# Routing stage of a Mamba, attention and mixture-of-experts block: inverse softmax sums spread by repeated DMA loads instead of by TensorE

## The chip, the cores and the metric

The kernel runs on one core of a Trainium2 chip. The metric is the time of one execution on the device in microseconds (us); lower is better. The time before is the median of three runs, 3432.8 us (3429.8 to 3436.05).

The core's engines are TensorE (PE in the profile, its weight loads PEld), VectorE (DVE), ScalarE (ACT), GpSimd (POOL) and SyncE (SP). SP's queue issues nearly all DMA transfers here; GpSimd's queue issues the indirect ones.

## The reference, cut to what matters

The input `x` is 2 batches of 2048 tokens of 256 channels. It is normalised, and goes through a Mamba block and through a transformer layer with a top-1 mixture of 8 experts; both results are added to `x`. The changed part lies in the transformer layer, between attention and the experts:

```python
attn = jax.nn.softmax(scores, axis=-1)
o = jnp.einsum('bhqk,bhkd->bhqd', attn, v)          # 16 heads of 16 channels
o = o.transpose(0, 2, 1, 3).reshape(b, s, h)
x = x + (o @ wo + bo)
hn2 = _layernorm(x, ln2_g, ln2_b).reshape(-1, h)
logits = hn2 @ gate_w + gate_b
idx = jnp.argmax(logits, axis=-1)                    # one expert for each token
...
moe = y[idx, jnp.arange(hn2.shape[0])]
return x + moe.reshape(b, s, h)
```

## The kernel before

Five stages follow each other, each closed by a barrier of all engines: projection of q, k and v; Mamba; attention; routing (`phase_route`, the changed function); experts.

**What attention leaves.** It works on items, one for each batch, group of 4 heads and block of 512 tokens: 2 x 4 x 4 = 32. For each item it writes a 128x512 block to `oraw_d` in DRAM: for each of the 4 heads 16 rows of unnormalised output and, in the seventeenth row, the softmax sums. Its end also loads the sums of the first 28 items (`SUMS_KEPT`), inverts them and stores them to `rs_d`, 4 rows of 512 for each item. The last 4 items (`LATE`) are left to the routing stage.

**Routing** handles 8 chunks of 512 tokens (`NCH`); `c` is the chunk. The channels are on the partitions (`OT[c]`, 128 partitions, 2 halves `k`, 512 tokens).

- SP, `load_o(c)` (L1398 to L1404): four DMAs of 128 KB, one for each half `k` and each group `g`, each from 4 heads x 16 rows x 512 to 64 partitions x 512. They signal `o_in[c % RING]`, `RING` being 4.
- SP, `load_inverses` (L1406 to L1410): one 32 KB DMA for each batch and group puts the stored inverses into `INV`, 16 partitions (one for each head). The four inverses of the late items are loaded as sums (`SS`), inverted by VectorE (L1626) and copied into `INV` by four small DMAs (L1424).
- TensorE, `spread(c)` (L1480 to L1489): two fp32 products of the selection matrix `SEL` (made by GpSimd, 1 where the channel belongs to the head) with `INV[:, c, :]` repeat each head's inverses over its 16 channels, in the PSUM tile `pS`. Each fp32 product shows as two matmul records.
- VectorE, `scale(c)` (L1574 to L1577): `OT[c] = pS * OT[c]`.
- TensorE, `project(c)` (L1491 to L1499): `OT[c]` times `WO` into `pA`.
- VectorE, `stats(c)` (L1579 to L1589): `pA` plus `XN[c]`, then mean and variance; `normalise(c)` gives `HN`.
- GpSimd, `base(c)` (L1461 to L1463): `XB[c] += XN[c]`, a 128x1024 tensor_tensor in SBUF.
- TensorE `turn` and `gate`, VectorE `choose` (L1601 to L1614): logits, largest logit, one-hot choice of expert. TensorE `count` and VectorE `place` (L1616 to L1622): the slot of each token in its expert's list.
- GpSimd, `scatter(c)` (L1465 to L1470): four indirect DMAs, each of which writes 128 token numbers of 4 bytes to computed slots of `ids_d`.
- SP stores `HN` to `hn_d` and `XB[c]` to `base_d`, 512 KB each in rows of 1 KB.

**Order.** Each engine's order is written out by hand. VectorE: scale(0), inversion of the late sums, then for each c: stats(c), place(c-2), scale(c+1), normalise(c), choose(c-1). TensorE: for each c: project(c+1), spread(c+2), turn(c), count(c-1), gate(c). GpSimd: base(c), scatter(c-1). SP: loads of chunks 0 to 2 (`AHEAD` is 3) with the inverses between them, a wait for the inverted late sums, then for each c: load_o(c+3), a wait for `hn_done` (c), store of `HN`, a wait for `base_done` (c), store of `XB`. The stage ends when all stores and scatters have landed.

Of the kernel before, what the change touches and what calls it, by code (L numbers as in the profile page):

```python
# [33 lines left out]
GH = 4  # L34
# [1286 lines left out]
def phase_route(nc, kept, oraw_d, rs_d, ids_d, hn_d, base_d, TE, TR, batches):  # L1321
# [11 lines left out]
    LATE = ITEMS - SUMS_KEPT  # L1333
    O_IN = 16 * 4
    AHEAD = 3
    with ExitStack() as ctx:
# [5 lines left out]
        OT = [m.sb(f"ot{c}", [P, KC, BANK]) for c in range(NCH)]  # L1342
        SEL = m.sb("sel", [HEADS, KC, P])
        INV = m.sb("inv", [HEADS, NCH, BANK])
        HN = [m.sb(f"hn{n}", [P, TG, C]) for n in range(2)]
# [15 lines left out]
        CMP = m.sb("cmp", [P, NTL, NE])  # L1361
        pA = m.ps("pA", [P, TG, C])
        pS = m.ps("pS", [P, KC, BANK])
        pT = [m.ps(f"pT{n}", [P, 2, KC, P]) for n in range(2)]
# [5 lines left out]
        inverted = m.sem("inverted")  # L1370
        inv_in = m.sem("inv_in")
        late_in = m.sem("late_in")
        s_ps = m.sem("s_ps")
        o_in = [m.sem(f"o_in{n}") for n in range(RING)]
# [19 lines left out]
        with nc.Block() as block:  # L1394

            @block.sync
            def _(sp):
                def load_o(c):  # L1398
                    b, cb = divmod(c, NB)
                    for k in range(KC):  # L1400
                        for g in range(2):
                            raw = oraw_d[b * GB * NB + (2 * k + g) * NB + cb].rearrange("(h r) q -> h r q", r=P // GH)
                            half = slice(g * GH * HD, (g + 1) * GH * HD)
                            sp.dma_start(OT[c][half, k, :], raw[:, 0:HD, :]).then_inc(o_in[c % RING], 16)  # L1404

                def load_inverses(b, g):  # L1406
                    first = (b * GB + g) * NB
                    sp.dma_start(INV[g * GH:(g + 1) * GH, b * NB:(b + 1) * NB, :],
                                 rs_d[first * GH:(first + NB) * GH, :].rearrange("(c h) q -> h c q", h=GH)
                                 ).then_inc(inv_in, 16)  # L1410

                sp.dma_start(SS[:, :], oraw_d[SUMS_KEPT:ITEMS].rearrange("i (h r) q -> (i h) r q", r=P // GH)[:, HD, :]
                             ).then_inc(sums_in, 16)
                for g in range(GB):
                    load_inverses(0, g)
                load_o(0)
                for b in range(1, batches):
                    for g in range(GB - (b == batches - 1)):
                        load_inverses(b, g)
                load_o(1)  # L1420
                load_o(2)
                sp.wait_ge(inverted, 1)
                for i in range(LATE):
                    sp.dma_start(INV[HEADS - GH:HEADS, NCH - LATE + i, :], SS[i * GH:(i + 1) * GH, :]  # L1424
                                 ).then_inc(late_in, 16)
                for c in range(NCH):
                    if c + AHEAD < NCH:
                        if c + AHEAD >= RING:
                            sp.wait_ge(scaled, c + AHEAD - RING + 1)
                        load_o(c + AHEAD)  # L1430
                    rows = slice(c * BANK, (c + 1) * BANK)
                    sp.wait_ge(hn_done, c + 1)
                    sp.dma_start(hn_d[rows, :].rearrange("(t p) c -> p t c", p=P), HN[c % 2][:, :, :]
                                 ).then_inc(hn_out[c % 2], 16)
                    sp.wait_ge(base_done, c + 1)
                    sp.dma_start(base_d[rows, :].rearrange("(t p) c -> p t c", p=P), XB[c][:, :, :]).then_inc(base_out, 16)
                for n in range(2):
                    sp.wait_ge(hn_out[n], 16 * (NCH // 2))
                sp.wait_ge(base_out, 16 * NCH)

            @block.gpsimd
            def _(pool):
                make_identity(pool, ident, id_ready)
                pool.memset(SEL[:, :, :], 1.0).then_inc(id_ready, 1)
                pool.wait_ge(id_ready, 3)
                pool.affine_select(out=SEL[:, :, :], in_=SEL[:, :, :], compare_op=ALU.is_gt, fill=0.0, base=1,
                                   pattern=[[P, KC], [1, P]], channel_multiplier=-HD).then_inc(id_ready, 1)
                pool.wait_ge(id_ready, 4)
                pool.affine_select(out=SEL[:, :, :], in_=SEL[:, :, :], compare_op=ALU.is_gt, fill=0.0, base=HD,
                                   pattern=[[-P, KC], [-1, P]], channel_multiplier=HD).then_inc(id_ready, 1)  # L1450
                pool.iota(IDT[:, :], pattern=[[P, NCH * TG]], base=0, channel_multiplier=1).then_inc(consts, 1)
# [27 lines left out]
            def _(pe):  # L1479
                def spread(c):  # L1480
                    if c >= 1:
                        pe.wait_ge(scaled, c)
                    if c == 0:
                        pe.wait_ge(inv_in, 16 * (GB * batches - 1))
                    if c == NCH - LATE:
                        pe.wait_ge(late_in, 16 * LATE)
                    for k in range(KC):
                        mm = pe.matmul(pS[:, k, :], SEL[:, k, :], INV[:, c, :], start=True, stop=True)
                    mm.then_inc(s_ps, 1)  # L1489

                def project(c):  # L1491
                    pe.wait_ge(scaled, c + 1)
                    if c >= 1:
                        pe.wait_ge(x1_done, c)
                    for t in range(TG):
                        for k in range(KC):
                            mm = pe.matmul(pA[:, t, :], OT[c][:, k, t * P:(t + 1) * P], WO[:, k, :],
                                           start=(k == 0), stop=(k == KC - 1))
# [30 lines left out]

                pe.wait_ge(id_ready, 5)  # L1530
                spread(0)
                project(0)
                spread(1)
                pe.wait_ge(consts, 8)
                for c in range(NCH):
                    if c + 1 < NCH:
                        project(c + 1)
                    if c + 2 < NCH:
                        spread(c + 2)
                    turn(c)  # L1540
# [20 lines left out]
            def _(dve):  # L1561
# [12 lines left out]
                def scale(c):  # L1574
                    dve.wait_ge(o_in[c % RING], O_IN * (c // RING + 1))
                    dve.wait_ge(s_ps, c + 1)
                    dve.tensor_tensor(OT[c][:, :, :], pS[:, :, :], OT[c][:, :, :], ALU.mult).then_inc(scaled, 1)  # L1577

                def stats(c):  # L1579
                    dve.wait_ge(a_ps, c + 1)  # L1580
                    dve.tensor_tensor(XN[c][:, :, :], pA[:, :, :], XN[c][:, :, :], ALU.add).then_inc(x1_done, 1)
                    dve.wait_ge(x1_done, c + 1)
# [383 lines left out]
```

## Time and profile before

| | |
|---|---|
| median of 3 runs | 3432.8 us (3429.8 to 3436.05) |
| the profiled execution | 3432.8 us |
| its span | 3431.2 us |
| TensorE busy | 2923.5 us, 85% |
| VectorE busy | 2602.2 us, 76% |
| ScalarE busy | 1711.8 us, 50% |
| GpSimd busy | 929.5 us, 27% |
| routing stage | 2939.1 to 3078.7 us |

The profile is one execution. Times within it are us from the start of its span. A row of the timeline gives start, duration, engine, line of the kernel, what is written and read, shape and count; what stands in brackets behind it is how long the engine was idle before it, and what ended that. The clock given with a window is the one granted to TensorE, as a share of full speed. The DMA share is the mean busy share of the core's 16 DMA engines; GB/s is what they moved together. A DMA's landing is the time from its issue to its last signal.

### The profile page before, as it was taken

The page shows a single profiled execution, that of the slowest core. Times are in us where ns is not written, and L with a number is a line of the kernel's source. Part 1 is how long each engine was busy: PE and PEld are TensorE (multiplying, and loading weights), DVE is VectorE, ACT ScalarE, POOL GpSimd, SP SyncE. Part 2 cuts the span into 40 slices and gives each one's busy share as a digit, 9 for nine tenths or more (in the row PEclk, how much of TensorE's full clock was granted, in tenths as well). Part 3 has the DMA queues.
Part 4 walks back from the last instruction along what each step waited for, and adds up shares of the span by engine and source line. Part 5 has one row for each costly group of instructions (what it writes and reads, how often), then busy time and mean ns, then how long its engine had stood idle before and what let it go on. Part 6 is the DMA issues. An engine that isn't in the chain of part 4 may idle for free. (4 is left out here: it accounts for less than half of the span.)

```text
span 3431.2 us, 42905 instructions
## 1 busy us (share of the span) xinstructions
PE 2923.5 (85%) x12700; PEld 1390.8 (41%) x12700; DVE 2602.2 (76%) x3764; ACT 1711.8 (50%) x2099; POOL 929.5 (27%) x530
## 2 busy tenths in 40 slices
PE   5768697897977877699899999999999999759998
PEld 3433243343433423333333333333333333448887
DVE  5426898998988999588898988889888996462222
ACT  2325545545546454056676766667666777211110
POOL 2203554555545556300000000000000000143443
PEclk9879899998999988689999999999999999769999
DMA  4542111212111111755445555435554430355663
GB/s 148 171 136 81 62 74 56 81 68 74 68 68 68 68 50 55 94 66 79 70 63 82 66 85 78 63 63 74 78 85 64 63 46 7 81 100 196 201 206 122
DMA packets 215985, 296.83 MB, mean 87 GB/s; under 512 B 117806, under 2 KB 162376, under 8 KB 201310
## 3 DMA queue, kind: packets, MB, share of 16 engines
q1 hardware_dynamic: 203262, 264.30, 35.8%
q0 software_dynamic: 12512, 29.82, 3.0%
q8 instruction: 120, 1.97, 0.3%
q14 instruction: 91, 0.75, 0.1%
HBM read 241.40 MB, written 57.56 MB: 87 GB/s over the span
## 5 line engine op out<-in xcount | busy, mean ns | idle before, releaser
L736 DVE TENSOR_REDUCE attn_mx<-attn_pX 128x1 f32<-128x512 f32 x2048 | 1271.8, 683 | 183.4 <-PE attn_pX L642 181.6
L714 ACT ACTIVATE attn_pr<-attn_pS 128x1024 f32<-128x1024 f32 x1024 | 992.6, 1022 | 524.1 <-PE attn_pS L655 523.4
L642 PE MATMUL attn_pX<-attn_ks,attn_qs 48*128 48x512 f32 x2048 | 754.1, 494 | 76.5 <-DMA attn_vs<-v_d 25.4
L1186 PE MATMUL mamba_pY<-mamba_g,mamba_ident 128*128 128x512 f32 x1024 | 530.5, 667 | 203.8 <-DVE mamba_g L1312 203.2
L1299 DVE TENSOR_TENSOR_SCAN mamba_h<-mamba_pA,mamba_hs,mamba_db 128x512 f32<-128x512 f32 x512 | 617.7, 1264 | 66.4 <-ACT mamba_pA L1045 65.7
L642 PEld LDWEIGHTS attn_pX<-attn_ks,attn_qs 48*128 48x128 f32 x2048 | 306.9, 192 | 780.0 <-DVE attn_mx L736 714.9
L1045 ACT ACTIVATE mamba_pA<-mamba_dt,mamba_an 128x512 f32<-128x512 f32 x512 | 351.7, 691 | 497.8 <-DVE mamba_h L1299 497.6
L982 POOL TENSOR_TENSOR mamba_db<-mamba_bq,mamba_u 128x2048 f32<-128x2048 f32 x128 | 579.3, 4526 | 71.3 <-DVE mamba_u L1259 71.0
L665 PE MATMUL attn_pO<-attn_pr,attn_vs 128*17 128x512 f32 x4096 | 556.6, 616 | 0.4 <-ACT attn_pr L714 0.4
L655 PE MATMUL attn_pS<-attn_qs,attn_ks 50*128 50x512 f32 x2048 | 471.4, 416 | 52.3 <-DMA attn_qs<-attn_mt 33.5
L1186 PEld LDWEIGHTS mamba_pY<-mamba_g,mamba_ident 128*128 128x128 f32 x1024 | 213.2, 214 | 504.5 <-DVE mamba_g L1312 260.0
L1312 DVE TENSOR_TENSOR mamba_g<-mamba_h,mamba_bq 128x2048 f32<-128x2048 f32 x128 | 294.0, 2297 | 7.8
L655 PEld LDWEIGHTS attn_pS<-attn_qs,attn_ks 50*128 50x128 f32 x2048 | 255.6, 192 | 90.9 <-issue 54.2
L623 POOL DMA_DIRECT2D rows_xn<-xn_d x8 | 6.1, 767 | 1018.1 <-PE attn_pO L665 1018.1
L1115 PE MATMUL mamba_pP<-mamba_xt,mamba_wc 128*128 128x512 f32 x512 | 227.0, 597 | 22.9 <-DVE mamba_an L1284 22.9
L1864 DVE TENSOR_SCALAR exp_hm<-exp_pH,exp_b 128x256 f32<-128x256 f32 x46 | 22.3, 484 | 234.6 <-PE exp_pH L1802 234.6
L1828 ACT ACTIVATE exp_hm<-exp_pH,exp_b 128x256 f32<-128x256 f32 x46 | 21.8, 475 | 320.7 <-PE exp_pH L1802 320.7
L1802 PE MATMUL exp_pH<-exp_xt,exp_w 128*128 128x256 f32 x736 | 165.0, 383 | 1.1 <-DVE exp_xt L1843 1.1
L1815 PE MATMUL exp_pY<-exp_w,exp_hm 128*128 128x256 f32 x736 | 162.7, 379 | 0.0
L1115 PEld LDWEIGHTS mamba_pP<-mamba_xt,mamba_wc 128*128 128x128 f32 x512 | 97.7, 191 | 147.9 <-issue 147.9
L966 POOL TENSOR_TENSOR mamba_hs<-mamba_h,mamba_mk 128x4 f32<-128x4 f32 x126 | 25.2, 200 | 483.8 <-DVE mamba_g L1312 483.8
L1802 PEld LDWEIGHTS exp_pH<-exp_xt,exp_w 128*128 128x128 f32 x736 | 141.4, 192 | 21.1 <-DVE exp_xt L1843 1.5
(190 smaller groups left out, 2076.2 us busy)
## 6 DMA issues: line engine op xcount, KB each, us to landing
mamba_bq<-bc_d SPq DMA_DIRECT2D x64, 1024.0 KB, 4.7
attn_ks<-parts_d SPq DMA_DIRECT2D x192, 256.0 KB, 8.7
exp_w<-in_w SPq DMA_DIRECT2D x46, 1024.0 KB, 5.5
attn_vs<-v_d SPq DMA_DIRECT2D x32, 544.0 KB, 15.6
parts_d<-proj_qp SPq DMA_DIRECT2D x32, 512.0 KB, 3.0
attn_qs<-parts_d SPq DMA_DIRECT2D x192, 64.0 KB, 8.3
attn_qs<-attn_mt SPq DMA_DIRECT2D x512, 1.0 KB
oraw_d<-attn_oe SPq DMA_DIRECT2D x32, 256.0 KB, 2.1
```

Source lines behind the costliest of these rows:

```text
L642: pe.matmul(pX[bank(s, n)][:, :], QS[slot][rows, pair, qt * P:(qt + 1) * P], KS[slot][rows, pair, part * BANK:(part + 1) * BANK], start=Tr ...
L655: mm = pe.matmul(pS[pair][:, h, :], KS[slot][rows, pair, kt * P:(kt + 1) * P], QS[slot][rows, pair, :], start=True, stop=True)
L665: mm = pe.matmul(pO[32 * h:32 * h + VW, :], VS[s][:, kt, h, :], PR[2 * (kt % 2) + h // 2][:, h % 2, :], start=(kt == 0), stop=(kt == KT - 1))
L714: act.activation(PR[2 * (kt % 2) + pair][:, :, :], pS[pair][:, :, :], ACT.Exp, scale=HD ** -0.5).then_inc(p_sb, 1)
L736: dve.tensor_reduce(MX[:, col:col + 1], pX[bank(s, n)][:, :], AX.X, ALU.max).then_inc(x_max, 1)
L982: pool.tensor_tensor(DB[k % 2][:, :, :], BQ[q % 2][:, 0, :, :], U[s][:, j, :].unsqueeze(1).to_broadcast([P, QN, BANK]), ALU.mult).then_inc ...
L1045: act.activation(pA[n % 2][:, :], DT[s][:, j, :], ACT.Exp, scale=AN[:, j, q * QN + n:q * QN + n + 1]).then_inc(da_done, 1)
L1115: mm = pe.matmul(bank(s, place)[0:rows, :], w, x, start=(i == 0), stop=(i == len(pairs) - 1))
L1186: mm = pe.matmul(pY[j][:, :], ident[:, :], G[k % 2][:, n, :], start=False, stop=(q == NQ - 1 and n == QN - 1))
L1299: dve.tensor_tensor_scan(H[k % 2][:, n, :], pA[n % 2][:, :], DB[k % 2][:, n, :], HS[:, j, q * QN + n:q * QN + n + 1], ALU.mult, ALU.add).t ...
L1312: dve.tensor_tensor(G[k % 2][:, :, :], H[k % 2][:, :, :], BQ[q % 2][:, 1, :, :], ALU.mult).then_inc(hc_done, 1)
L1802: mm = pe.matmul(pH[n][:, f % 2, :], W1[s][:, k, f * P:(f + 1) * P], XT[s][:, k, :], start=(k == 0), stop=(k == KC - 1))
```

## The change

- `load_inverses`, `INV`, `SEL`, the PSUM tile `pS`, `spread` and the four small copies of late inverses are gone.
- A new `load_r(c)` on SP's queue: four DMAs for each chunk, one for each half `k` and group `g`. Each reads the 4 rows of inverses of one item from `rs_d`, repeats each 16 times (a stride of zero in the second dimension) and writes 64 partitions x 512, 128 KB, into a new SBUF tile `SM[c]`. They signal the same semaphore as `load_o(c)`, so scale waits for eight DMAs (`O_IN = 16 * 8`).
- The late sums are inverted in `SS` as before, and then stored to `rs_d` by one 32 KB DMA. SP waits for it before `load_r(4)`, the first chunk of batch 1.
- `scale(c)` is `OT[c] = OT[c] * SM[c]`, both operands in SBUF.
- SP loads 2 chunks ahead instead of 3. The load of the late sums comes after the eight DMAs of chunk 0 instead of first.
- `pA` has two buffers, and `project(c)` waits for the sum of chunk c-2 instead of c-1.

```diff
@@ phase_route, constants and tiles
     LATE = ITEMS - SUMS_KEPT
-    O_IN = 16 * 4
-    AHEAD = 3
+    O_IN = 16 * 8
...
-        SEL = m.sb("sel", [HEADS, KC, P])
-        INV = m.sb("inv", [HEADS, NCH, BANK])
+        SM = [m.sb(f"sm{c}", [P, KC, BANK]) for c in range(NCH)]
...
-        pA = m.ps("pA", [P, TG, C])
-        pS = m.ps("pS", [P, KC, BANK])
+        pA = [m.ps(f"pA{n}", [P, TG, C]) for n in range(2)]
@@ SP
-                def load_inverses(b, g):
-                    first = (b * GB + g) * NB
-                    sp.dma_start(INV[g * GH:(g + 1) * GH, b * NB:(b + 1) * NB, :],
-                                 rs_d[first * GH:(first + NB) * GH, :].rearrange("(c h) q -> h c q", h=GH)
-                                 ).then_inc(inv_in, 16)
-
+                def load_r(c):
+                    b, cb = divmod(c, NB)
+                    for k in range(KC):
+                        for g in range(2):
+                            i = b * GB * NB + (2 * k + g) * NB + cb
+                            half = slice(g * GH * HD, (g + 1) * GH * HD)
+                            sp.dma_start(SM[c][half, k, :], rs_d[i * GH:(i + 1) * GH, :].unsqueeze(1)
+                                         .to_broadcast([GH, HD, BANK])).then_inc(o_in[c % RING], 16)
+
+                load_o(0)
+                load_r(0)
                 sp.dma_start(SS[:, :], oraw_d[SUMS_KEPT:ITEMS].rearrange("i (h r) q -> (i h) r q", r=P // GH)[:, HD, :]
                              ).then_inc(sums_in, 16)
-                for g in range(GB):
-                    load_inverses(0, g)
-                load_o(0)
-                for b in range(1, batches):
-                    for g in range(GB - (b == batches - 1)):
-                        load_inverses(b, g)
                 load_o(1)
-                load_o(2)
+                load_r(1)
                 sp.wait_ge(inverted, 1)
-                for i in range(LATE):
-                    sp.dma_start(INV[HEADS - GH:HEADS, NCH - LATE + i, :], SS[i * GH:(i + 1) * GH, :]
-                                 ).then_inc(late_in, 16)
+                sp.dma_start(rs_d[SUMS_KEPT * GH:ITEMS * GH, :], SS[:, :]).then_inc(inv_out, 16)
                 for c in range(NCH):
-                    if c + AHEAD < NCH:
-                        if c + AHEAD >= RING:
-                            sp.wait_ge(scaled, c + AHEAD - RING + 1)
-                        load_o(c + AHEAD)
+                    if c + 2 < NCH:
+                        if c + 2 >= RING:
+                            sp.wait_ge(scaled, c + 3 - RING)
+                        load_o(c + 2)
+                        if c + 2 == NB * (batches - 1):
+                            sp.wait_ge(inv_out, 16)
+                        load_r(c + 2)
@@ GpSimd
-                pool.memset(SEL[:, :, :], 1.0).then_inc(id_ready, 1)
...
@@ TensorE
-                def spread(c):
...
-                    for k in range(KC):
-                        mm = pe.matmul(pS[:, k, :], SEL[:, k, :], INV[:, c, :], start=True, stop=True)
-                    mm.then_inc(s_ps, 1)
-
                 def project(c):
                     pe.wait_ge(scaled, c + 1)
-                    if c >= 1:
-                        pe.wait_ge(x1_done, c)
+                    if c >= 2:
+                        pe.wait_ge(x1_done, c - 1)
@@ VectorE
                 def scale(c):
                     dve.wait_ge(o_in[c % RING], O_IN * (c // RING + 1))
-                    dve.wait_ge(s_ps, c + 1)
-                    dve.tensor_tensor(OT[c][:, :, :], pS[:, :, :], OT[c][:, :, :], ALU.mult).then_inc(scaled, 1)
+                    dve.tensor_tensor(OT[c][:, :, :], OT[c][:, :, :], SM[c][:, :, :], ALU.mult).then_inc(scaled, 1)
```

## Rows read from the trace of the kernel before

**Rows 1.** The page: busy time, a load of the mamba stage

```profile
PE 2923.5 (85%) x12700; PEld 1390.8 (41%) x12700; DVE 2602.2 (76%) x3764; ACT 1711.8 (50%) x2099; POOL 929.5 (27%) x530
...
mamba_bq<-bc_d SPq DMA_DIRECT2D x64, 1024.0 KB, 4.7
```

**Rows 2.** Windows inside the routing stage: start:end, length, busy us (instructions), clock, DMA, GB/s

```profile
core 0: us, PE busy (x) PEld busy (x) DVE busy (x) ACT busy (x) POOL busy (x), PEclk, DMA share, GB/s
2936.00:2955.00 19.00, 3.75 (x4) 1.16 (x4) 0.54 (x4) 1.28 (x1) 2.27 (x10) 0.60 0.28 95
3000.00:3045.00 45.00, 41.50 (x178) 31.80 (x177) 42.41 (x123) 7.13 (x18) 24.93 (x20) 0.77 0.70 113
2970.00:2973.00 3.00, 3.00 (x11) 1.97 (x10) 0.80 (x1) 0.00 (x0) 0.00 (x0) 0.92 1.02 335
```

**Rows 3.** Waits in the routing stage: line, what it waited for, us, times, longest

```profile
PE route_pS L1488 <- DMA route_inv<-rs_d: 15.7, 1, 15.7
DVE route_ot L1577 <- PE route_pS L1488: 15.2, 1, 15.2
```

**Rows 4.** Timeline of the routing stage: start us, us, engine, line, work [idle before]

```profile
2950.81 3.75 PE L1488 MATMUL route_pS<-route_inv,route_sel 16*128 16x512 f32 x4 [15.73 <-DMA route_inv<-rs_d]
...
2954.66 1.23 DVE L1577 TENSOR_TENSOR route_ot<-route_pS,route_ot 128x1024 f32<-128x1024 f32 x1 [15.24 <-PE route_pS L1488]
...
2987.06 1.23 DVE L1577 TENSOR_TENSOR route_ot<-route_pS,route_ot 128x1024 f32<-128x1024 f32 x1
...
3036.96 1.22 DVE L1577 TENSOR_TENSOR route_ot<-route_pS,route_ot 128x1024 f32<-128x1024 f32 x1
...
3038.24 5.41 PE L1497 MATMUL route_pA<-rows_wo,route_ot 128*128 128x256 f32 x16
...
3041.68 2.92 DVE L1610 TENSOR_TENSOR route_oh<-route_wtt,route_mw 128x32 f32<-128x32 f32 x1
3042.17 2.36 POOL L1463 TENSOR_TENSOR rows_xb<-rows_xb,rows_xn 128x1024 f32<-128x1024 f32 x1
```

**Rows 5.** Timeline of the end of the routing stage

```profile
3045.51 1.22 DVE L1581 TENSOR_TENSOR rows_xn<-route_pA,rows_xn 128x1024 f32<-128x1024 f32 x1
...
3062.79 0.17 DVE L1622 CAST route_slot<-route_slf 128x4 int32<-128x4 f32 x1
...
3078.70 0.21 POOL L92 MEMSET exp_ident<- 128x128 f32 x1 [10.68 <-POOLq L1394]
```

**Rows 6.** DMA of 2944 to 2959 us: busy tenths in slices, total, issues

```profile
DMA  2232222222222222222222222222222222222222
...
DMA packets 760, 1.45 MB, mean 97 GB/s; under 512 B 54, under 2 KB 54, under 8 KB 759
...
route_ot<-oraw_d SPq DMA_DIRECT2D x8, 128.0 KB
```

**Rows 7.** Timeline of SP's DMA issues in the routing stage

```profile
2939.14 0.34 SPq L1412 DMA_DIRECT2D route_ss<-oraw_d  x1
...
2990.67 0.36 SPq L1433 DMA_DIRECT2D hn_d<-route_hn  x1
...
3007.53 10.73 SPq L1404 DMA_DIRECT2D route_ot<-oraw_d  x4
...
3032.07 0.36 SPq L1436 DMA_DIRECT2D base_d<-rows_xb  x1
```

**Rows 8.** DMA issues near 2969, 2990 and 3032 us: count, KB, us to landing

```profile
hn_d<-route_hn SPq DMA_DIRECT2D x1, 512.0 KB, 3.0
base_d<-rows_xb SPq DMA_DIRECT2D x1, 512.0 KB, 4.4
...
hn_d<-route_hn SPq DMA_DIRECT2D x1, 512.0 KB, 17.1
...
base_d<-rows_xb SPq DMA_DIRECT2D x1, 512.0 KB, 8.0
```

**Rows 9.** Groups of instructions, page part 5: busy us, mean ns, idle before

```profile
L1312 DVE TENSOR_TENSOR mamba_g<-mamba_h,mamba_bq 128x2048 f32<-128x2048 f32 x128 | 294.0, 2297 | 7.8
```

More of the change, by code:

```diff
@@ L1370, in phase_route @@
         inverted = m.sem("inverted")
-        inv_in = m.sem("inv_in")
-        late_in = m.sem("late_in")
-        s_ps = m.sem("s_ps")
+        inv_out = m.sem("inv_out")
         o_in = [m.sem(f"o_in{n}") for n in range(RING)]
@@ L1443, in _ @@
                 make_identity(pool, ident, id_ready)
-                pool.memset(SEL[:, :, :], 1.0).then_inc(id_ready, 1)
[L1445 to L1450, printed above, removed]
                 pool.iota(IDT[:, :], pattern=[[P, NCH * TG]], base=0, channel_multiplier=1).then_inc(consts, 1)
@@ L1479, in _ @@
             def _(pe):
-                def spread(c):
-                    if c >= 1:
[L1482 to L1486, printed above, removed]
-                    for k in range(KC):
-                        mm = pe.matmul(pS[:, k, :], SEL[:, k, :], INV[:, c, :], start=True, stop=True)
-                    mm.then_inc(s_ps, 1)
                 def project(c):
                     pe.wait_ge(scaled, c + 1)
-                    if c >= 1:
-                        pe.wait_ge(x1_done, c)
+                    if c >= 2:
+                        pe.wait_ge(x1_done, c - 1)
                     for t in range(TG):
                         for k in range(KC):
-                            mm = pe.matmul(pA[:, t, :], OT[c][:, k, t * P:(t + 1) * P], WO[:, k, :],
+                            mm = pe.matmul(pA[c % 2][:, t, :], OT[c][:, k, t * P:(t + 1) * P], WO[:, k, :],
                                            start=(k == 0), stop=(k == KC - 1))
@@ L1528, in count @@
                     pe.matmul(pN[:, c % 2, 0:TG, :], LOWER[:, :], OH[:, :, :], start=False, stop=True).then_inc(n_ps, 1)
-                pe.wait_ge(id_ready, 5)
-                spread(0)
                 project(0)
-                spread(1)
+                pe.wait_ge(id_ready, 2)
                 pe.wait_ge(consts, 8)
@@ L1537, in _ @@
                         project(c + 1)
-                    if c + 2 < NCH:
-                        spread(c + 2)
                     turn(c)
@@ L1575, in scale @@
                     dve.wait_ge(o_in[c % RING], O_IN * (c // RING + 1))
-                    dve.wait_ge(s_ps, c + 1)
-                    dve.tensor_tensor(OT[c][:, :, :], pS[:, :, :], OT[c][:, :, :], ALU.mult).then_inc(scaled, 1)
+                    dve.tensor_tensor(OT[c][:, :, :], OT[c][:, :, :], SM[c][:, :, :], ALU.mult).then_inc(scaled, 1)
                 def stats(c):
                     dve.wait_ge(a_ps, c + 1)
-                    dve.tensor_tensor(XN[c][:, :, :], pA[:, :, :], XN[c][:, :, :], ALU.add).then_inc(x1_done, 1)
+                    dve.tensor_tensor(XN[c][:, :, :], pA[c % 2][:, :, :], XN[c][:, :, :], ALU.add).then_inc(x1_done, 1)
                     dve.wait_ge(x1_done, c + 1)
```

## The prediction

> **What bounds the kernel now.** I read the page first, for the shares of the engines and to find the stage [rows 1]. The changed function is the routing stage, from 2939.1 us, where SP issues its first load [rows 7], to 3078.7 us, where the expert stage begins [rows 5]: 140 us of 3431. Everything behind it starts when it ends, so a shift of its end moves the end of the kernel one for one, if the stages on either side keep their length; they are not touched.
>
> Second, the list of waits. Multiplying the raw attention output by the inverse sums (scale, L1577) waits once, 15.2 us, and TensorE's spreading of the inverses (L1488) waits once, 15.7 us, for the loads of the inverses [rows 3]. After the first chunk scale is never late for data.
>
> Third, the timeline. scale starts at 2954.66, the fourth at 2987.06 and the eighth at 3036.96 [rows 4]: 49.9 us for four chunks, 12.5 us each. In that stretch VectorE is busy 42.4 of 45 us and the DMA engines 70% [rows 2], so VectorE sets the pace, with DMA close behind. Part of its busy time is a stall: a 128x32 operation at L1610 shows 2.92 us while GpSimd runs a 2.36 us tensor_tensor beside it [rows 4]. From the last scale to the last slot (L1622) it is 25.8 us, and from there to the next stage 15.9 us [rows 4, 5]: scatter, its landing, the barrier.
>
> Fourth, the DMA view, which decides this case. From 2944 to 2959 us, loads of raw output are queued back to back, and yet the sixteen engines are busy only two to three tenths and carry 97 GB/s [rows 6]. When the stores of a chunk flow, from 2970 to 2973 us, all engines are busy and carry 335 GB/s [rows 2]. With twelve loads queued the share does not rise, so these loads share the same quarter of the engines, four of them, and go one behind another. A 128 KB load costs 131 KB / 97 GB/s = 1.35 us, a chunk of four 5.4 us. The Trainium skill (DMA: Bandwidth & Descriptors, on why a DMA increments its semaphore by 16) says the number of engines is the largest up to 16 that divides the outermost sizes of both sides, and that they are the lowest-numbered; here the source's outermost size is 4 heads. The trace's quarter share agrees.
>
> **The change, part by part.**
>
> Removed on TensorE: 32 spreading matmuls and their selection matrix. TensorE is not what VectorE waits for after the first chunk [rows 3], so its gain is nothing, hidden under VectorE. Removed from DMA: seven 32 KB loads of inverses and four of 8 KB; at 97 GB/s the seven are 7 x 0.34 = 2.4 us.
>
> Moved on VectorE: scale takes both operands from SBUF. L1312, two SBUF operands of 2048 elements, takes 2.30 us [rows 9]; half the elements are near the 1.22 us that scale takes now [rows 4]. I take no difference; the bounds are 0 and +1.1 us per chunk, of which only the last chunk's counts if DMA sets the pace. Such a scale may meet GpSimd's 2.36 us operation, but L1610 pays for that today, and one operation pays for it either way. A second accumulator in PSUM frees project from the sum before it; no wait on that is among those that matter, so nothing.
>
> Added on DMA: for each chunk, four more loads of 128 KB, each four rows of inverses repeated sixteen times, 32 in all. Their source has the same outermost 4 and their target the same 64 partitions as the loads of raw output. I price them alike, 1.35 us on the same four engines. The nearest row the other way is the broadcast load of the mamba stage, 1 MB in 4.7 us [rows 1], which uses all engines, but its outermost size is the 128 partitions; it shows that repeated reads of a row are not slow or especially cheap. The rule of the Trainium skill cited above would put the new loads on four engines too; by it the sum is the one below, and by the mamba row it would be that of the second rival.
>
> Sum on the four engines, in the order of SP's queue. First, the latency that isn't transfer: the wait for inverses ends at 2950.81 [rows 4], 11.7 us after the first issue at 2939.14 [rows 7]; in between lie four loads of output (5.4) and seven of inverses (2.4), so 3.9 us are start and completion. In the changed kernel the eight loads of chunk 0 land at 2939.1 + 3.9 + 8 x 1.35 = 2953.8, 0.9 us ahead of today's first scale. The loads of chunk 7 stand behind 56 others and behind the stores of chunks 0 to 4, because SP's program issues chunk c+2's loads before chunk c's stores. The stores of a chunk are 2 x 524 KB / 335 GB/s = 3.1 us on every engine [rows 2]; undisturbed they land in 3.0 and 4.4 us [rows 8]. So chunk 7 lands at 2939.1 + 3.9 + 64 x 1.35 (86.4) + 5 x 3.1 (15.5) + 0.3 for the two 32 KB transfers of sums = 3045.2, against 3036.96: +8.2 us. The pace, 10.8 + 3.1 = 13.9 us, is now DMA's, not VectorE's 12.5. A prefetch of two chunks instead of three costs nothing more, since the queue of the four engines is never empty.
>
> The tail: VectorE no longer lags behind. Today the eighth x + projection (L1581) starts 8.55 us after its scale, 2.7 of it the stall at L1610. With 1.3 us for scale and 5.4 for the projection [rows 4] it could start after 6.9 us: -1.6 us, bounds -1.7 and 0. Undisturbed sum: +6.6 us.
>
> Disturbed: the stores slow down once the indirect scatter (L1468) is under way. Chunk 2's store, issued at 2990.67, takes 17.1 us, and chunk 5's, issued at 3032.07, lands 8.0 us later, at 3040.1 [rows 7, 8]. In these 49.4 us the four engines carry four pairs of stores (12.5) and two chunks' loads (10.8), 23.3 us of work: 26 us too much, up to 6.5 per pair. SP too is held: four issues last 10.7 us from 3007.53 [rows 7]. In the changed kernel the pairs of chunks 1 to 4 reach the four engines just when the loads of a chunk have landed, about 14 us after the previous ones; the slots of an earlier chunk are ready some 12 us after its landing, so scatter and stores meet four times. Bounds 0 and 4 x 6.5 = 26 us. I take about half, 3.4 us each, +13.6, because twelve of sixteen engines will have done their stores earlier and a scatter comes once in 17 us instead of 12.5. Total +20 us.
>
> Queued behind SP's longer issue are the stores; normalise waits for a store two chunks back, which lies ahead of the loads that normalise's predecessor already waited for, so no new wait. The new wait of SP for the stored late inverses comes before chunk 4, some 30 us after that store; free.
>
> The profiled execution is 3432.8 us, 1.6 above its span and equal to the median of the runs. **Forecast 3453 us**, own range 3443 to 3466 (+10 to +33).
>
> **The rivals.** Bound for all: 0.2%, 6.9 us, is about what a measurement of this kernel tells from no change.
> A. Stores and scatter don't add: only the undisturbed sum, +5 to +9, 3440 us. For it: twelve engines write earlier than today. Against: chunk 2's 17.1 us [rows 8].
> B. Faster: the repeated rows go over all sixteen engines, as the mamba broadcast does. A chunk's loads are then 5.4 + 1.35 = 6.8 us, chunk 0 lands at 2949.8, 4.9 us earlier than today's first scale, and VectorE's 12.5 us pace again decides, as long as loads, stores and disturbance stay under it: chunk 7 lands at 2939.1 + 3.9 + 54.4 + 15.8 + at most 26 = 3039 at the latest, 3026 at half. -5 to -6 us with the tail, 3427 us. Against: the outermost size.
> C. No change: the sixteen reads of one row cost under 0.98 us per load, so a chunk is 5.4 + 3.9 + 3.1 < 12.5 us and VectorE keeps the pace; start and pace as today, 3433 us. Against: 1 MB in 4.7 us gives no rate above the usual one.
> D. The disturbance grows with the traffic, reads included: above +33, 3470 us.
>
> **Numbers.** Forecast 0.62, A 0.12, B 0.08, C 0.08, D 0.10. A straddles the bound, 0.07 slower and 0.05 same. Slower 0.79, same 0.13, faster 0.08. The range 3436 to 3468 leaves out B, C and part of D.
>
> **What would show it.** In the changed profile: scale waits for a DMA at nearly every chunk; DMA from 2941 to about 2965 us stays at a quarter share and 97 GB/s; scale starts at 2954, then every 14 us and more after the fourth; VectorE's busy share in the stage falls; TensorE has no L1488 work. Wrong would be: a share well above a quarter in the first 20 us (B), scale intervals of 12.5 us (B or C), or of 13.9 us throughout (A).

## The result, and the profile after

The changed kernel takes 3466.8 us (median of 4 runs, 3464.8 to 3471.9), the kernel before, run beside it, 3434.4 us (3429.8 to 3438.9). The ratio is 1.0097, 95% interval 1.0079 to 1.0115: slower by 32.4 us. The profiled execution of after took 3471.8 us (span 3470.2), 39.0 us more than that of before. Of this, 4.0 us lie ahead of the changed stage, in code that is the same: its first load is issued at 2943.14 us instead of 2939.14. The stage itself is 174.9 us long instead of 139.6: +35.3 us. From here on a start is told after the stage's first issue ("rel."), so that the 4.0 us do not get in the way.

Rows of the timeline of after that answer to [rows 4, 5] (start, us, engine, line, work, idle before and releaser):

```profile
2956.90 1.23 DVE L1549 TENSOR_TENSOR route_ot<-route_ot,route_sm 128x1024 f32<-128x1024 f32 x1 [13.47 <-DMA route_sm<-rs_d]
...
2967.69 1.23 DVE L1549 TENSOR_TENSOR route_ot<-route_ot,route_sm 128x1024 f32<-128x1024 f32 x1 [0.56 <-DMA route_sm<-rs_d]
...
2990.26 1.07 POOL L1456 DMA_INDIRECT ids_d<-route_idt,route_slot  x1 [10.98 <-DVE route_slot L1594]
...
2991.75 1.23 DVE L1549 TENSOR_TENSOR route_ot<-route_ot,route_sm 128x1024 f32<-128x1024 f32 x1 [1.79 <-DMA route_sm<-rs_d]
...
3023.76 1.23 DVE L1549 TENSOR_TENSOR route_ot<-route_ot,route_sm 128x1024 f32<-128x1024 f32 x1 [19.23 <-DMA route_sm<-rs_d]
...
3074.35 3.75 DVE L1549 TENSOR_TENSOR route_ot<-route_ot,route_sm 128x1024 f32<-128x1024 f32 x1 [4.79 <-DMA route_sm<-rs_d]
3074.67 2.35 POOL L1451 TENSOR_TENSOR rows_xb<-rows_xb,rows_xn 128x1024 f32<-128x1024 f32 x1
...
3084.80 1.22 DVE L1553 TENSOR_TENSOR rows_xn<-route_pA,rows_xn 128x1024 f32<-128x1024 f32 x1 [2.17 <-PE route_pA L1474]
...
3102.09 0.17 DVE L1594 CAST route_slot<-route_slf 128x4 int32<-128x4 f32 x1
...
3117.99 0.21 POOL L92 MEMSET exp_ident<- 128x128 f32 x1 [10.67 <-POOLq L1389]
```

The first four scales come 10.8, 11.5 and 12.5 us apart (rel. 13.8, 24.6, 36.1, 48.6; before 15.5, 26.3, 36.7, 47.9 by the same reading). Then there are 32.0 us to the fifth, and VectorE idles 19.23 us of it for a load. The first scatter of slots, at 2990.26, stands just ahead of this gap. The last row of scale is three times as long as the others, beside GpSimd's operation of 2.35 us.

The waits of the stage, against [rows 3]:

```profile
PE route_pA L1474 <- DVE route_ot L1549: 76.8, 8, 21.9
...
DVE route_ot L1549 <- DMA route_sm<-rs_d: 51.2, 7, 19.2
```

Seven of eight scales wait for the repeated loads, 51.2 us in all, where before one waited, for TensorE. Windows of the stage, against [rows 2] (the last one has the limits of the window shown there):

```profile
core 0: us, PE busy (x) PEld busy (x) DVE busy (x) ACT busy (x) POOL busy (x), PEclk, DMA share, GB/s
2943.00:2962.00 19.00, 3.82 (x11) 3.18 (x12) 4.71 (x6) 1.28 (x1) 1.21 (x7) 0.52 0.25 87
2962.00:2992.00 30.00, 19.33 (x91) 16.02 (x89) 19.71 (x66) 4.48 (x11) 6.13 (x4) 0.83 0.42 152
2992.00:3023.00 31.00, 9.82 (x44) 8.21 (x44) 11.81 (x35) 2.14 (x5) 11.18 (x9) 0.61 0.34 70
...
3000.00:3045.00 45.00, 17.59 (x87) 15.03 (x86) 20.00 (x66) 4.28 (x10) 12.52 (x10) 0.66 0.35 98
```

From 3000 to 3045 VectorE was busy 42.4 us before and is 20.0 us now; the DMA engines' share fell too, from 0.70 to 0.35. In the gap (2992 to 3023) loads are queued all the time, and only 70 GB/s move, less than half of the stretch ahead of it. So the stage waits for DMA while DMA moves little and is not out of work. The DMA view of 2944 to 2962 us (against [rows 6]) and of 2992 to 3004 us:

```profile
DMA  0301222222244222222222222222222222222222
...
DMA packets 872, 1.66 MB, mean 92 GB/s; under 512 B 64, under 2 KB 64, under 8 KB 871
```

```profile
DMA  3222591129800000101911900500000001080004
GB/s 96 96 96 102 94 61 48 61 77 41 14 0 1 0 0 0 24 24 34 55 48 41 14 7 27 20 0 0 0 0 14 21 27 34 27 27 27 20 27 14
DMA packets 380, 0.40 MB, mean 33 GB/s; under 512 B 109, under 2 KB 266, under 8 KB 380
...
hn_d<-route_hn SPq DMA_DIRECT2D x1, 512.0 KB, 26.4
```

The first is the quarter share of four engines with repeated loads among the others. The second is what adding up bandwidths does not show: a third of that rate, with slices near nothing, and a store that lands after 26.4 us. SP is held as well (timeline of SP around that stretch, against [rows 7]):

```profile
2985.47 5.76 SPq L1399 DMA_DIRECT2D route_ot<-oraw_d  x4
2991.28 7.32 SPq L1407 DMA_DIRECT2D route_sm<-rs_d  x4
2998.64 7.11 SPq L1428 DMA_DIRECT2D hn_d<-route_hn  x1
3005.80 9.85 SPq L1431 DMA_DIRECT2D base_d<-rows_xb  x1
3015.69 7.39 SPq L1399 DMA_DIRECT2D route_ot<-oraw_d  x4
```

The first two rows are the eight loads of the fifth chunk (chunk 4). SP has issued the last of them by 2998.60, and the fifth scale starts at 3023.76, 25 us later. So this gap does not come from a late issue, though the scatters stand ahead of `base` in GpSimd's order, and SP waits for `base`.

### The profile page after: what moved, and what is told of

Read it like the earlier page. It is cut to its first block and busy times, and to the rows that moved or that the text cites. A ratio compares the mean times of both kernels' runs of the same rounds, so it can differ in the third digit from the quotient of the medians.

```text
span 3470.2 us, 42850 instructions
## 1 busy us (share of the span) xinstructions
PE 2911.1 (84%) x12668; PEld 1388.7 (40%) x12668; DVE 2599.9 (75%) x3764; ACT 1710.9 (49%) x2099; POOL 927.4 (27%) x527
## 5 line engine op out<-in xcount | busy, mean ns | idle before, releaser
L982 POOL TENSOR_TENSOR mamba_db<-mamba_bq,mamba_u 128x2048 f32<-128x2048 f32 x128 | 579.3, 4526 | 73.1 <-DVE mamba_u L1259 72.8
L1115 PEld LDWEIGHTS mamba_pP<-mamba_xt,mamba_wc 128*128 128x128 f32 x512 | 97.9, 191 | 147.2 <-issue 147.2
## 6 DMA issues: line engine op xcount, KB each, us to landing
attn_vs<-v_d SPq DMA_DIRECT2D x32, 544.0 KB, 15.5
```

The costliest lines, as they stand in the source:

```text
L982: pool.tensor_tensor(DB[k % 2][:, :, :], BQ[q % 2][:, 0, :, :], U[s][:, j, :].unsqueeze(1).to_broadcast([P, QN, BANK]), ALU.mult).then_inc ...
L1115: mm = pe.matmul(bank(s, place)[0:rows, :], w, x, start=(i == 0), stop=(i == len(pairs) - 1))
```

## The experiments

All starts are in us after the stage's first issue; "tail" is from the eighth scale to the first instruction of the next stage. Each median stands against runs of the kernel before on the same chip: 3434.4 us for after, 3438.7 for r16 to late_after, 3439.0 for b_ahead1 to r16_ahead3, 3441.9 for shift to distinct. The ratio is an estimate of its own and not quite the quotient of the two medians (or16: 1.0131 against 1.0145). The times within the stage are from one profiled execution of each kernel.

| kernel | median us | ratio to before (95%) | first scatter | longest gap between scales | eighth scale | tail |
|---|---|---|---|---|---|---|
| before | | | 48.3 | 12.5 | 97.8 | 41.7 |
| after | 3466.8 | 1.0097 (1.0079 to 1.0115) | 47.1 | 32.0, 4th to 5th | 131.2 | 43.6 |
| r16 | 3457.3 | 1.0052 (1.0030 to 1.0074) | 44.3 | 34.2, 4th to 5th | 121.7 | 41.9 |
| or16 | 3488.5 | 1.0131 (1.0105 to 1.0157) | 57.9 | 34.8, 3rd to 4th | 152.3 | 40.2 |
| ahead3 | 3467.0 | 1.0079 (1.0058 to 1.0099) | 46.9 | 31.4, 4th to 5th | 131.4 | 41.9 |
| late_after | 3468.1 | 1.0084 (1.0062 to 1.0106) | 112.5 | 13.8 | 102.1 | 68.3 |
| b_ahead1 | 3479.9 | 1.0124 (1.0101 to 1.0146) | 57.3 | 32.9, 4th to 5th | 144.0 | 40.3 |
| late_before | 3464.0 | 1.0064 (1.0048 to 1.0081) | 107.1 | 13.2 | 95.1 | 73.1 |
| no_r | 3442.6 | 1.0010 (0.9998 to 1.0022) | 42.2 | 28.4, 5th to 6th | 106.1 | 41.1 |
| r16_ahead3 | 3455.1 | 1.0046 (1.0030 to 1.0063) | 44.5 | 24.8, 4th to 5th | 119.3 | 42.8 |
| shift | 3476.4 | 1.0107 (1.0085 to 1.0129) | 60.1 | 36.5, 5th to 6th | 134.4 | 43.9 |
| late_store | 3469.1 | 1.0089 (1.0067 to 1.0111) | 46.1 | 30.1, 4th to 5th | 116.6 | 58.8 |
| plain4 | 3507.2 | 1.0191 (1.0173 to 1.0210) | (plain) | 25.8, 4th to 5th | 128.4 | 86.9 |
| distinct | 3488.0 | 1.0137 (1.0113 to 1.0160) | 47.1 | 39.9, 4th to 5th | 150.8 | 43.6 |

**r16 and or16: the loads over all engines.** In r16 a repeated load is cut by head, so that 32 partitions and not 4 rows are its outermost size:

```diff
-   sp.dma_start(SM[c][half, k, :], rs_d[i * GH:(i + 1) * GH, :].unsqueeze(1)
-                .to_broadcast([GH, HD, BANK])).then_inc(o_in[c % RING], 16)
+   for h in range(GH):
+       part = slice((g * GH + h) * HD, (g * GH + h + 1) * HD)
+       sp.dma_start(SM[c][part, k, :], rs_d[i * GH + h:i * GH + h + 1, :]
+                    .to_broadcast([HD, BANK])).then_inc(o_in[c % RING], 16)
```

or16 cuts the loads of the raw output by head too.

> The changed kernel with each repeating load cut into four, one head each (1 row repeated to 16 partitions, outermost size 16); same bytes, same rows, same packets. Theory Q (four engines carry all loads one behind another): these loads spread over all sixteen engines, the four busiest have 5.4 + 1.35 + 3.1 = 9.9 us of work per chunk, VectorE's 12.5 us pace returns; total within -6 to +12 us of before, most of the 32 us gone. Rival R (sixteen reads of the same row are slow in themselves): total stays +20 to +35. Rival S (scale with two SBUF operands, blocked by GpSimd): stays +20 or more.

> As r16, and the loads of raw output cut by head as well: 32 DMAs of 32 KB per chunk, all with outermost size 16. Theory Q: 2.7 us per chunk on every engine, no loads queue up on four; the limit becomes SP's issuing, 32 x 0.33 = 10.6 us per chunk, still under 12.5; total -8 to +8 us of before. Rival R: +20 to +35.

In r16 the first four scales start at 11.6, 22.7, 33.3 and 45.3, 33.7 us for three intervals against 34.8 in the changed kernel, and 2.2 us sooner; then the same gap comes. The total is 18.6 us over before, between the two ranges that were expected. In or16 a chunk has 32 loads, and SP issues one in about 0.46 us: 14.7 us per chunk, and 15.3 is the pace from the first scale on. Cutting finer moved the bound from the four engines to SP. The total, 49.8 us over before, is above both expected ranges: SP's pace had been priced at 10.6 us per chunk, and the gap of 34.8 us behind the first scatter not at all.

**ahead3: three chunks ahead instead of two.** `load_o(2); load_r(2)` are issued ahead of the loop, and the loop loads chunk c+3.

> The changed kernel, loads issued three chunks ahead instead of two. Theory Q: the queue of the four engines is never empty either way, so no difference from the changed kernel: +27 to +38 us. Rival P (the shorter prefetch is what costs): +0 to +12 us.

The eighth scale starts at 131.4 against 131.2, and the total is 28.2 us over before, as the first theory expected. One chunk more of depth is no help here.

**late_after and late_before: the scatters behind everything else.** The same edit on either kernel:

```diff
                 for c in range(NCH):
                     base(c)
-                    if c >= 1:
-                        scatter(c - 1)
-                scatter(NCH - 1)
+                for c in range(NCH):
+                    scatter(c)
```

> The changed kernel, all 32 indirect scatters after the last base instead of one chunk's after each. Theory Q with disturbance by the scatter: eighth scale about 106 us after the first issue of the stage instead of 131, intervals of 13.9 us from the third on; the 41 us of scatters then stand at the end, so the total is about +25 us. If the disturbance comes from the stores alone: eighth scale stays at 125 us or later and the total goes to +45 us.

> The kernel before with all scatters issued after the last base. Theory S: its loads were never in the scatters' way, so the eighth scale moves by less than 2 us from 97.8, the 1 KB store packets of chunks 1 to 7 are quick again (landings of 3 to 5 us instead of 8 to 21), and the scatters that were hidden now stand in the tail: total 10 to 30 us over before (in the change the same move left the total where it was, and 29 us were won ahead of the tail). Rival (the scatters cost the kernel before time in its chunks too): the eighth scale is more than 3 us early.

This pair carries the verdict. Without scatters among its loads the changed kernel has no gap at all: scales at 13.5, 24.4, 35.8, 48.4, 61.7, 75.5, 88.8 and 102.1, the eighth 29.1 us sooner than in after. In the kernel before the same edit wins 2.7 us (97.8 to 95.1), which lies between the under 2 us of the one expectation and the over 3 us of the other. Both totals gain nothing by it, since 32 scatters, one in 1.27 us, now stand behind the last base: the tails grow by 24.7 and 31.4 us. DMA view of late_after from 2990 to 3012 us, about where after had its gap:

```profile
DMA  2224994228982222222222222222599322898222
GB/s 101 101 104 166 395 382 171 101 97 317 384 309 97 97 97 101 97 99 95 93 97 97 99 106 101 101 104 101 209 389 369 121 97 101 313 391 302 97 104 89
DMA packets 2830, 3.73 MB, mean 170 GB/s; under 512 B 115, under 2 KB 1907, under 8 KB 2829
```

Loads at a quarter share and near 97 GB/s, broken by stores at 9 tenths and up to 395 GB/s, and nothing else: this is the undisturbed queue that the prediction added up.

**b_ahead1: the kernel before, one chunk ahead.** `AHEAD = 1`, and the loads of chunks 1 and 2 are no longer issued ahead of the loop. No repeated load is in it.

> The kernel before, but each chunk's rows are asked for one chunk ahead instead of three, so that the loads of chunks 4 to 7 fall behind the first scatter instead of ahead of it. Theory S (what costs the change its time is that its loads run while the scatters of slots write, and the kernel before is spared since its loads are over by then): scales 1 to 4 stay within 2 us of the kernel before (they start 26.3, 36.7, 47.9 and 60.4 us after the first issue), and those after the first scatter come late, the eighth 10 to 30 us later than 97.8; total 3445 to 3470. Theory V (it is the volume: the change moves twice the bytes, and the scatter matters only to a queue that is already full): loads of 5 us per chunk have room for themselves, the eighth scale starts within 5 us of 97.8; total within 0.2% of before.

Its gap of 32.9 us opens at the first scatter and its scale now waits for the load of the raw output (summary of line L1575 of b_ahead1; the kernel before had no such wait [rows 3]):

```profile
L1575 DVE TENSOR_TENSOR route_ot<-route_pS,route_ot x8: 1223/1225/1225, 2957.4 to 3085.8; 128x1024 f32<-128x1024 f32 x8
its engine sat idle before it (us, times) until:
  DMA route_ot<-oraw_d: 45.5, 7
```

So the collision needs no repeated load, and was there to be had in the kernel before. Two parts of the expectation failed. The first four scales did not keep their times: the fourth starts at 59.7 instead of 47.9, so 11.8 of the 46.2 us by which the eighth is late are the shorter prefetch alone, ahead of any scatter. And the total is above its range (3445 to 3470). Nor does this run show what the scatters hit first: between the first one and the fifth scale, 63 of the 1024 store packets of 1 KB take over 1 us (152 of their 228 us), and 11 of the 332 load packets of 2 KB (18 of 52 us). What spared the kernel before is slack: its loads for chunk 6 are issued at 2995.2 us and first used at 3024.5, 29 us later.

**no_r: the changed kernel without its repeated loads.** SM is set to one by VectorE ahead of the first scale, and `load_r` issues nothing, so that the softmax division is left out.

> The changed kernel without its repeated loads: SM is set to one by VectorE ahead of the first scale, so the softmax division is left out of what the stage computes. It keeps the SBUF operand of the scale, the second tile for the project's sums and the prefetch of two chunks. Theory S: only 32 loads remain (5.4 us a chunk on four engines), those of chunks 4 to 7 still partly behind the first scatter, so the eighth scale starts 97 to 112 us after the first issue; total 3430 to 3450. Theory V (volume alone): 95 to 98, total 3427 to 3435, at or under before. If what costs is the SBUF operand or the shared port, the total stays near the changed kernel's 3467.

The total is that of before within the measurement. The first scale comes 6.6 us sooner than before (8.9), the gap is still there, now 28.4 us from the fifth to the sixth. Half of the load bytes are gone, and the gap is hardly shorter (28.4 against 32.0): it is not a matter of volume alone. The SBUF operand of scale and the second accumulator are still there, so they are not what costs the 32 us. And even for nothing the division would not have made this stage shorter (147.2 us against 139.6). Without the division the tokens' experts can be others, and so the slots that the scatters write to; no run keeps these the same.

**r16_ahead3.** r16 with the edit of ahead3.

> The repeated loads cut by head over 16 engines (pace 11 to 12 us per chunk before the first scatter, measured) with three chunks ahead instead of two. Theory S: the loads of chunk 4 are now over before the first scatter, the gap moves from chunk 4 to a later one and shrinks, the eighth scale starts 100 to 118 us after the first issue instead of 121.7; total 3440 to 3457. Theory P (the gap belongs to chunk 4 whatever was loaded when, for example by the rows that it reads): the fifth scale starts about 30 us after the fourth as it did with two ahead; total near 3457.

The total is in the expected range, but the gap did not move to a later chunk as expected. It is still between fourth and fifth and is 24.8 us instead of 34.2; later ones of 16.2 and 20.7 leave the eighth scale at 119.3 against 121.7, and 3455.1 us against 3457.3 is no difference that these runs tell.

**shift: each scatter two chunks later.** `if c >= 3: scatter(c - 3)` in the loop, and the last three behind it.

> The changed kernel with each scatter of slots issued two chunks later (after the base of chunk c+3 instead of c+1). Theory S (a gap opens in the scales when the first scatter starts, since the loads then in flight crawl): the long gap moves with the scatter, from between the fourth and fifth scales to between the fifth and seventh, and is again 20 to 35 us; the eighth scale starts 115 to 135 us after the first issue; total 3460 to 3475. Theory P (the gap belongs to chunk 4: its rows, its wait for the late inverses): the fifth scale still starts over 28 us after the fourth.

The fifth scale starts 13.3 us after the fourth, at 61.6; the gap, 36.5 us, comes between fifth and sixth, behind the first scatter at 60.1. The gap belongs to the scatter, not to chunk 4, whose loads stand behind a wait of SP. The total, 3476.4 us, is 1.4 above the expected range.

**late_store: no stores among the loads.** Eight hn tiles instead of two, and SP issues all stores of hn and base behind the last load.

> The changed kernel with all stores of hn and base issued after the last load (eight hn tiles instead of two), the scatters where they are. Theory S1 (the scatters slow the loads directly): the fifth scale still starts over 25 us after the fourth, and the eighth 120 us or later; total 3470 to 3495, with the stores in the tail. Theory S2 (the scatters slow the 1 KB stores, and the loads only stand behind them in the same queue): no gap over 18 us, the eighth scale at 100 to 108 us; total 3445 to 3470.

The gap is 30.1 us with no store in flight. The eighth scale, at 116.6, is sooner than the 120 of the first theory, and the total, 3469.1, just under its range; later gaps are only 12.7 to 14.9. DMA view of its gap, 2984 to 3012 us; the first scatter is issued at 2982.7:

```profile
DMA  2222226900000030104333119007500000031122
GB/s 94 100 99 94 97 94 85 24 0 0 0 0 0 20 9 0 15 29 56 53 30 6 9 41 56 0 0 44 18 0 0 0 0 12 32 26 18 44 94 85
DMA packets 749, 0.97 MB, mean 35 GB/s; under 512 B 278, under 2 KB 278, under 8 KB 749
...
route_ot<-oraw_d SPq DMA_DIRECT2D x4, 128.0 KB
route_sm<-rs_d SPq DMA_DIRECT2D x4, 128.0 KB
ids_d<-route_idt,route_slot POOLq DMA_INDIRECT x8, 12.5
```

Eight loads and eight scatters are all that is issued. The loads run at 97 GB/s for 4 us, and then at 35 on the mean, with stretches of nothing. The scatter hits the loads themselves; with the stores among them the later gaps are longer (14.3, 20.8 and 15.6 us in after).

**plain4: direct four-byte writes in the scatters' place.** The scatters are as in late_after, and in the loop stands

```diff
+   pool.dma_start(decoy_d[t * P:(t + 1) * P, :], IDT[:, t:t + 1]).then_inc(decoyed, 16)
```

> The changed kernel with the scatters moved behind the last base as before, and in their old place direct DMAs of the same queue that write the same 512 four-byte elements per chunk to a scratch in order. Theory W (what collides is many four-byte writes of GpSimd's queue, indirect or not): the gap between the fourth and fifth scales is back (over 25 us), the eighth scale at 120 us or later; total 3480 to 3500. Theory I (it is the indirect form): no gap, the eighth scale at 100 to 106 us as with the scatters simply moved; total 3466 to 3475.

The gap is back, 25.8 us, and the eighth scale starts at 128.4 against late_after's 102.1. So the indirect form is not needed: 512 direct writes of four bytes for each chunk, on GpSimd's queue, do it. The total is 7.2 us above the range expected for this theory: the tail is 86.9 us, against 68.3 in late_after.

**distinct: as many different rows.** The second load reads rows of the attention's output, the same ones as `load_o`, so that the scale multiplies by those instead of by the inverses:

```diff
-   sp.dma_start(SM[c][half, k, :], rs_d[i * GH:(i + 1) * GH, :].unsqueeze(1)
-                .to_broadcast([GH, HD, BANK])).then_inc(o_in[c % RING], 16)
+   raw = oraw_d[i].rearrange("(h r) q -> h r q", r=P // GH)
+   sp.dma_start(SM[c][half, k, :], raw[:, 0:HD, :]).then_inc(o_in[c % RING], 16)
```

> The changed kernel with its second loads reading as many distinct rows of the attention's output in place of one inverse row repeated 32 times, so that the scale multiplies by those instead of the softmax inverses. Theory Q (four engines carry each 128 KB load, whatever rows it reads): scales 13 to 14 us apart before the gap, share of the engines 0.25 and total within 0.3% of the changed kernel's 3467. Rival C (repeated reads of one row have a price or a saving of their own): the pace before the gap differs by over 1 us a chunk.

Up to the fourth scale (48.6 in both) it makes no difference which rows are read, as long as there are no scatters; that half of the expectation held. The total did not: ratio 1.0137 against the changed kernel's 1.0097, some 14 us more, with gaps of 39.9 and 34.8 us. Under the scatters, this kernel's loads are delayed more than those of the changed kernel. What makes the difference is not shown. It need not be the rows read: with other values the tokens' experts can be others too, and so the slots that the scatters write to.

## Why the prediction was right, and where it missed

**Direction and the four engines: right.** The repeated loads run on a quarter of the engines (share 0.25 and 87 GB/s in the window of the first 19 us, 92 GB/s from 2944 to 2962), scale waits for DMA seven times, VectorE's pace is gone. That the share follows how a load is cut, and not the bytes, is shown by the windows of the first 17 us, of after and of r16:

```profile
2943.00:2960.00 17.00, 1.82 (x4) 1.51 (x5) 3.30 (x5) 1.28 (x1) 1.21 (x7) 0.50 0.24 86
```

```profile
2943.00:2960.00 17.00, 4.87 (x12) 3.92 (x13) 4.51 (x3) 0.49 (x1) 0.58 (x4) 0.50 0.40 105
```

In r16, where only the repeated loads are cut finer, the share is 0.40 instead of 0.24.

**The queue's sum: right in kind, 4 us too dear.** Undisturbed (late_after) the eighth scale starts at 102.1; the prediction had 106.1. Against 97.8 in the kernel before the queue costs +4.3 us, where +8.2 was forecast. The pace under a full queue is 13.3 to 13.8 us against 13.9, and a prefetch of two instead of three costs nothing, as predicted (ahead3). Of the 4.0 us that are over in the sum, 1.2 lie ahead of the first scale (13.5 instead of 14.7) and 1.3 in the interval to the fourth (12.6 instead of 13.9); the rest is spread over the later intervals.

**The disturbance: the step that was mis-sized.** It was a term of +13.6 us (bounds 0 and 26), and it measures 131.2 - 102.1 = +29.1 us, above its upper bound. The bound was taken from four meetings of up to 6.5 us, each charged to a pair of stores. But the scatter delays the loads as well (late_store), and the first meeting alone opens a gap of 32.0 us where the pace is 13.3: 18.7 us, three times the bound of one meeting. The mechanism was stated as stores and scatter that meet; rival D had "reads included", for over +33 us, and in mechanism D is nearer than the forecast. The trace of before held a sign of it. Chunks 6 and 7 have 512 load packets of 2 KB, none of them run from 2990 to 3001 us, and all of them from 3001 to 3031 (DMA view of before; under 8 KB less under 2 KB):

```profile
DMA packets 3553, 3.72 MB, mean 124 GB/s; under 512 B 465, under 2 KB 3039, under 8 KB 3551
```

They take 30 us where the prediction's price is 10.8, with stores among them. Scale did not feel it, since these loads are issued 29 us ahead of their use, so the trace showed that loads slow down, but not what that costs when they are needed at once.

**The tail: wrong in sign.** Forecast -1.6 us, measured 43.6 - 41.7 = +1.9. From the eighth scale to the sum behind it (L1553) it takes 10.45 us, not 6.9. The stall beside GpSimd is not gone, it went to scale: 3.75 us instead of 1.23, beside the 2.35 us of L1451. It was said that one operation pays for it either way, and then only the saving was booked. Other profiles have it on other instructions behind an eighth scale of 1.23 us: in r16 and distinct the four of normalise take 4.26 us together, 1.38 elsewhere, and from the eighth scale to the sum it is 8.66 us, as good as the 8.55 of before. Where nothing meets, in late_after, it is 6.56 us, and the forecast 6.9 would have held.

**Scale from SBUF: right.** 1.23 us against 1.22.

**Removed TensorE work, the new wait of SP: right, both nothing.** Scale no longer waits for TensorE, and what the start gains (first scale at 13.8 instead of 15.5) is gone by the fourth (48.6 against 47.9); shift shows that chunk 4 as such has no gap.

**The total.** In the profiled stage the three terms are +4.3, +29.1 and +1.9, together +35.3 us, where +8.2, +13.6 and -1.6 were forecast. The median, 3466.8 us, is inside the range (3436 to 3468) by 1.2 us and 0.8 us outside the forecast's own range (3443 to 3466): +32.4 us on the kernel before as run beside it, where +20 was forecast. That it is inside is in part luck: the queue, 4 us too dear, makes up for some of the disturbance, which was beyond its bound.

**Rivals.** B (all engines) is refuted for this kernel by the share, and as a hope by r16: even with the repeated loads spread, the kernel is slower than before, 1.0052. C (repeated reads are cheap) is refuted by distinct, in the stretch without scatters, and by the pace of 13.3 to 13.8 us in late_after. A (no disturbance) is refuted by the gap; late_after shows what is left of it ahead of the tail, +4.3 us.

**Still open.** Why four-byte writes hold up other queues' packets. The traces show it as single long packets: in late_after and late_before no packet of 1 or 2 KB of the stretch from 2990 to 3040 us takes over 0.5 us, and the median is 0.05 and 0.08 us; in after, between the first scatter and the fifth scale, 22 of 570 packets of 2 KB take over 1 us, up to 7.5, and 60 of the 114 us that these packets take together. Over four engines, 60 us are 15 us each, an estimate that would be most of the 18.7 us by which this gap exceeds the pace. Whether the hold-up is in the memory's writing of so few bytes, or in how GpSimd's queue makes its descriptors, no run here tells apart. The Trainium skill (DMA: Bandwidth & Descriptors, on back-pressure in remote DMA) says that stalled writes also stall the other queues of the engine that they come from. It says so of transfers between cores; if it held here too, a few slow writes would be enough to hold the loads. The runs here do not contradict it, and none of them isolates it. Four-byte writes from SP's queue were not tried. No version tried beats the kernel before.

## What to carry to other kernels

A load that is hidden today has a price only when it is made to arrive later: read how long ahead of its use each load is issued, and what starts within that slack. Where a small scattered write runs beside a stream, do not price the stream from a stretch without it, or from one where its loads have slack; make the run that parts them, here one line moved. And a fix of the number of engines per load (r16) should be reckoned together with the issuing queue, whose 0.46 us per DMA became the bound in or16.

## What the runs showed of the hardware that was not expected

- Four-byte writes of GpSimd's queue, 512 per chunk, slow what the other queue moves to about a third (33 GB/s over 12 us in after, 35 over 28 us in late_store, instead of 97), with single 2 KB load packets of up to 7.5 and 7.6 us, where the median is 0.08. With direct instead of indirect writes (plain4) such packets reach 5.2 us, and the gap is 25.8 us.
- The kernel whose second loads read distinct rows loses more by it than the one with repeated rows (gaps of 39.9 and 34.8 us against 32.0 and 20.8), although both run alike up to the first scatter. The cause is not shown.
- SP is held in the issue of a single DMA for up to 10.6 us (a store in shift; 9.85 in after) while the queues ahead are slow. In late_after, without scatters among the loads, none is held for over 3.03 us.
- GpSimd's operation of 2.35 us stretches the VectorE instruction that meets it: scale in after (3.75 instead of 1.23 us), normalise in r16 (4.26 instead of 1.38). Moving work moved the stall.
